# Fourth layer's stack put in order by ScalarE in 16 pieces instead of by two GpSimd copies

## The reference

```
q, k, v = (qkv[:, :, 0], qkv[:, :, 1], qkv[:, :, 2])          # (n, t, h, d)
attn = jnp.einsum('nthd,ntkd->nthk', q * scale, k)            # 16 x 16 for each token
attn = jax.nn.softmax(attn, axis=-1)
out = jnp.einsum('nthk,ntkd->nthd', attn, v)
out = out.transpose(0, 2, 1, 3).reshape(n, t, d)
```

## Time and profile before

| | |
|---|---|
| median of 3 runs | 1935.79 us (1934.92 to 1936.99) |
| the profiled execution | 1931.41 us, span 1929.6 us |
| PE busy | 1609.7 us (83%) |
| DVE busy | 1265.1 us (66%) |
| ACT busy | 934.0 us (48%) |
| POOL busy | 382.1 us (20%), of it 112.4 us in 16 copies of line 571 |
| mean granted clock of TensorE | 0.875 of full speed |

### The profile page before, as it was taken

One profiled execution on the slowest core, in us unless ns is written; L12 is line 12 of the kernel. 1 busy time (PEld: TensorE's weight loads), 2 busy tenths in 40 slices (PEclk: granted clock), 3 DMA queues, 4 the chain that ended last, 5 costly groups with the idle time before them and its releaser, 6 DMA issues. The chain is left out here.

```text
span 1929.6 us, 37580 instructions
## 1 busy us (share of the span) xinstructions
PE 1609.7 (83%) x13794; PEld 1045.1 (54%) x13794; DVE 1265.1 (66%) x3174; ACT 934.0 (48%) x2095; POOL 382.1 (20%) x432
## 2 busy tenths in 40 slices
PE   7357977977888999999898998989878777977888
PEld 4124544554455666666666666656555455555556
DVE  5664666576577767666767767676676677566743
ACT  0124445544555555555555556555444444443544
POOL 1020111011021111111111111111331434143310
PEclk9957777878899999998989989899788789787978
DMA  6150331232144433333333434343675777557530
GB/s 175 49 142 21 95 81 40 69 94 58 38 116 102 100 94 97 95 95 92 97 91 98 97 98 100 92 102 92 52 104 89 80 64 105 89 71 66 109 10 25
DMA packets 198009, 163.22 MB, mean 85 GB/s; under 512 B 80108, under 2 KB 182004, under 8 KB 191684
## 3 DMA queue, kind: packets, MB, share of 16 engines
q1 hardware_dynamic: 189444, 153.14, 40.7%
q10 hardware_dynamic: 8384, 7.69, 1.4%
HBM read 98.05 MB, written 61.95 MB: 83 GB/s over the span
## 5 line engine op out<-in xcount | busy, mean ns | idle before, releaser
L1052 DVE TENSOR_REDUCE maxima<-score_bank 128x4 f32<-128x512 f32 x512 | 339.3, 686 | 141.1 <-PE score_bank L1338 140.4
L777 ACT ACTIVATE p_room<-st_bank 128x512 f32<-128x512 f32 x512 | 299.4, 597 | 231.5 <-PE st_bank L1363 146.4
L1363 PE MATMUL st_bank<-stack_room 64*128 64x128 bf16 x2048 | 243.9, 234 | 43.6 <-DMA stack_room<-max_T 25.6
L1363 PEld LDWEIGHTS st_bank<-stack_room 64*128 64x128 bf16 x2048 | 147.2, 101 | 203.2 <-issue 138.7
L1421 PE MATMUL lin<-h2T,w_h 128*128 128x256 f32 (+1 forms) x640 | 223.3, 444 | 30.6 <-ACT h2T L667 17.6
L835 ACT ACTIVATE gelu<-lin 128x256 f32<-128x256 f32 (+1 forms) x320 | 119.0, 382 | 264.2 <-PE lin L1421 264.2
L1338 PE MATMUL score_bank<-stack_room 62*128 62x128 bf16 x2048 | 201.7, 227 | 8.5 <-DVE maxima L1052 5.8
L563 POOL TENSOR_TENSOR part_low<-qk_rest,part_mid 96x512 bf16<-96x512 f32 x96 | 116.9, 1218 | 437.8 <-DVE part_mid L1038 437.8
L1447 PE MATMUL lin<-w_f,gelu 128*128 128x144 f32 (+1 forms) x1280 | 190.0, 296 | 0.0
L1074 DVE RECIPROCAL o_recip<-o_bank 128x16 f32<-128x16 f32 x128 | 32.8, 256 | 234.6 <-PE o_bank L1391 234.6
L549 POOL TENSOR_TENSOR rstd<-var,neg_half 128x2 f32<-128x2 f32 (+1 forms) x96 | 77.1, 803 | 534.3 <-DVE var L912 299.3
(11 more groups left out here) (194 smaller groups left out, 2719.1 us busy)
## 6 DMA issues: line engine op xcount, KB each, us to landing
stack_room<-stack_dram SPq DMA_DIRECT2D x96, 512.0 KB, 7.6
gates<-gates_dram SPq DMA_DIRECT2D x64, 288.0 KB, 4.3
stack_dram<-part_high SPq DMA_DIRECT2D x64, 288.0 KB, 3.1
norm_room<-stack_dram SPq DMA_DIRECT2D x32, 512.0 KB, 8.1
stack_dram<-part_mid SPq DMA_DIRECT2D x64, 192.0 KB, 2.6
stack_dram<-part_high SPq DMA_DIRECT2D x64, 144.0 KB, 3.2
stack_dram<-part_mid SPq DMA_DIRECT2D x64, 96.0 KB, 2.8
stack_dram<-part_low SPq DMA_DIRECT2D x64, 96.0 KB, 2.1
```

Of the source, the lines that this page charges most:

```text
L777: eng.activation(probs[:, i % PBUFS, :], st_bank[i % 2][:, :], ACT.Exp, scale=float(HD) ** -0.5)\
L1052: eng.tensor_reduce(maxima[:, b, CH * c:CH * c + CH], score_bank[i % 2][:, :].rearrange("p (h k) -> p h k", h=CH), AX_X, ALU.max)\
L1363: ins = eng.matmul(o, score_columns(1, g, b, c, j, HALF), score_columns(0, g, b, c, j, HALF), start=True, stop=flow_of(g) == "a")
```

## The change

GpSimd's `reorder` is deleted. ScalarE gets one that does the same permutation in 16 pieces, 8 for each of the two tiles: a piece takes 16 of the 128 values of m with all 32 of c, that is one run of 512 elements of stage, and writes them to the stack 256 bytes apart (the next m goes 2 bytes further). Pieces 0 to 7 of group L run in body(g): one after each of the five GELUs of half h = 1, and three at the end of the body behind the two `copy_max`. Pieces 8 to 15 run in the next body, one in each of the attention steps 0, 1, 5, 7, 10, 11, 13 and 15. Each piece first waits that the stage of its group is loaded. The stack that they write was last read by group g = L - 2, whose shifted scores are all done before its GELUs. The counts of `reordered` and the waits on it go from 2 to 16.

```diff
+PIECES = 8
-    "v_mixed": 2, "reordered": 2,
+    "v_mixed": 2, "reordered": 2 * PIECES,
@@ SP, load_stack
-                need(eng, "reordered", L - 1, 1)
+                need(eng, "reordered", L - 1, 2 * PIECES - 1)
@@ GpSimd
-            def reorder(J):
-
-                need(eng, "stack_loaded", J, STACK_LOADS - 1)
-                need(eng, "st_done", J - 2, STEPS - 1)
-                for s in range(2):
-                    eng.tensor_copy(stack[J % 2][s].rearrange("p (c m) -> p c m", m=TOK),
-                                    stage[s].rearrange("p (m c) -> p c m", m=TOK)).then_inc(S["reordered"], 1)
-                if J < NG and flow_of(J) == "t":
-                    reorder(J)
@@ ScalarE
+            def reorder(g, pieces):
+
+                need(eng, "stack_loaded", g, STACK_LOADS - 1)
+                n = TOK // PIECES
+                for i in pieces:
+                    k, s = divmod(i, 2)
+                    eng.activation(stack[g % 2][s].rearrange("p (c m) -> p m c", m=TOK)[:, k * n:(k + 1) * n, :],
+                                   stage[s].rearrange("p (m c) -> p m c", m=TOK)[:, k * n:(k + 1) * n, :], ACT.Copy)\
+                       .then_inc(S["reordered"], 1)
@@ ScalarE, attention(g)
+                rest = iter(range(PIECES, 2 * PIECES) if g + 1 < NG and flow_of(g + 1) == "t" else ())
+                    if i in (0, 1, 5, 7, 10, 11, 13, 15):
+                        for piece in rest:
+                            reorder(g + 1, [piece])
+                            break
@@ ScalarE, body(g): behind each GELU, and at the end
+                        if h == 1 and L < NG and flow_of(L) == "t":
+                            reorder(L, [T])
+                if L < NG and flow_of(L) == "t":
+                    reorder(L, range(FCT, PIECES))
@@ PE, scores
-                    need(eng, "reordered", g, 1)
+                    need(eng, "reordered", g, 2 * PIECES - 1)
```

## The result

The changed kernel takes 2051.6 us in the median (2046.7 to 2060.6), the kernel before 1936.4: a ratio of 1.059 (95% interval 1.054 to 1.064), slower by 115 us. Forecast were 1870 us, with a range of 1840 to 1912. The profiled execution took 2060.6 us, span 2058.9.

What follows compares the result with a forecast made beforehand. Layer 3's bodies (65.0 us, no engine full) were taken as bound by a VectorE cast held by GpSimd's copies. Savings of 48, 4 and 14 us less 0.5 gave 1865.9, plus 4.4 for the median: 1870 us, range 1840 to 1912.

Steps and rivals of the forecast that it cites:

- The hold: In layer 3's bodies with copies, GpSimd's two copies hold a VectorE cast 9.6 to 12.5 us; the change removes this.
- The body without additions: A layer 3 body without the copies, before ScalarE's added work: 22 us to exponential 15 plus 28.4, 50.4 us.
- The price of a piece: Each of 128 ScalarE copies of 512 elements: 0.62 us alone, 0.5 in a row, at most 1.04.
- The third rival: Pieces dearer still, kernel slower than before from about 1.1 us a piece; 1978 us at 1.46; chance 0.06.
- The rule of the 16-byte line: Skill text cited against the 0.62 us: writes going to a new SBUF line with each element should be slower.
- the doubled price: Second rival: ScalarE's pieces cost 1.04 us, 0.95 in a row, giving 1912 us; chance 0.25.
- The chain and the wait: SP's values, parts and stage loads end 47.2 us into a body; ScalarE waits 3.4 us; bodies 57 us.
- The clock: PE's granted clock in layer 3's bodies was to rise above 0.83.

Runs made afterwards that it cites:

- e5: The kernel before with GpSimd's two copies cut down to 8 elements each, nothing added on ScalarE (stack not put in order): 1817.7 us, ratio 0.940.
- e2: The changed kernel with each of the 16 pieces writing its 512 elements in a row (stack not put in order): 1880.0 us, ratio 0.972 to the kernel before.
- e8: The changed kernel with each piece writing its 512 elements in a row, run once more for its profile: 1863.6 us.
- e9: The changed kernel with two neighbours of the stack written one after the other within each piece: 1874.0 us, ratio 0.967 to the kernel before.

## Why the prediction was wrong

**The hold: right.** In the kernel after, the casts take 174 ns and PE doesn't wait at the flip, and in e5 exponential 0 to 15 takes 22.6 us (1519.72 to 1542.35) where I took 22. The body without additions was to be 50.4 us, and 51.0 were measured.

**The price of a piece: the step that failed.** The sum took 0.62 us for a piece and bounded it by 1.04 "from above"; it is 2.51. The upper end was built as twice ACT's time for an element, and that is what a jump costs in a read or in float32 (1.06 to 1.13). For single bf16 writes it isn't an upper end at all, and no row of the trace bore on them: GpSimd's 1.72 ns an element, which I set beside it, came from reads 64 bytes apart with writes in a row, and line 667's runs of 16 are the case that is free. I read both as evidence on a write that neither makes. The third rival, slower from about 1.1 us a piece and 1978 us at 1.46, was the right mechanism with a chance of 0.06. By its own sum with the measured price, 128 x (2.51 - 0.62) = 242 us on 1870, nothing hidden, it would have given 2112; 2052 were measured, so a part was hidden. With the same pieces at 0.62 to 0.68 us (e2, e8, e9) the kernel takes 1864 to 1880: the price alone turned the sign.

**The rule of the 16-byte line: right in direction, in part wrong in detail.** The Trainium skill, "Advanced Engine Details and Errata", section "SBUF Cachelines", says that going to another 16-byte line with each access costs a penalty, and that two hits on a line absorb the access time. It names no price; the doubling was mine. The traces agree for reads and float32 writes (0.69 us at 8 bytes apart, 1.13 at 16) and for pairs (0.63 to 0.67). They differ for single bf16 writes: at 8 bytes apart two of them hit each line, and they cost 1.38 us against 0.66 in a row. That the page speaks against this change deserved more than 0.25, and that the range ended at the doubled price was the error that no row excused.

**The chain and the wait: right in sum by luck.** At the price taken, bodies took 57.3 us (57 forecast), but not as forecast. ACT waited 1.1 to 1.7 us for the stage in four of those six bodies of e8 and not at all in the other two, where I had 3.4 in each. Its attention part took 27.8 us in body(27) (1600.12 to 1627.93), and 26.5 to 28.1 in the others, instead of my 24.2. The two errors cancel. Against e5's 22.6 us the added work cost some 5 us there and not the 2.2 that I gave it, and so the work came almost as late as the DMA. In body(23) ACT waited 6.4 us. In the kernel after, the wait came once, 2.2 us: pieces four times as long leave nobody early.

**The clock: wrong in direction.** I had counted on a clock above 0.83, and it fell to 0.67. One body of the kernel after in four stretches (columns as in rows 1): the end of the MLP, the last products and first scores, PE's wait, and what follows.

```profile
1683.00:1695.00 12.00, 8.98 (x45) 5.58 (x45) 5.32 (x12) 11.21 (x10) 0.79 (x1) 0.75 0.01 1
1695.00:1702.90 7.90, 7.90 (x55) 6.15 (x54) 3.92 (x8) 6.33 (x7) 1.31 (x5) 0.50 0.00 0
1702.90:1710.90 8.00, 0.06 (x2) 0.05 (x1) 0.00 (x0) 7.95 (x7) 0.00 (x0) 0.50 0.36 111
1710.90:1723.00 12.10, 11.58 (x91) 7.79 (x91) 5.47 (x13) 8.71 (x12) 0.00 (x0) 0.50 0.55 14
```

PE is at the lower of its two levels already ahead of the wait of 7.9 us, behind the GELUs where pieces leave it idle for a quarter of the time, and stays there through the wait and the 12 us behind it. PE's busy time for six bodies is 378.5 us against 276.1 in e5, for the same products. How much of that 102 us lies on the path no run separates.

## What to carry to other kernels

Price an access pattern by both of its sides and by its type: on this chip a bf16 write of single elements, 16 bytes or more apart, cost about four times a write in a row on ScalarE, GpSimd and VectorE (2.5 us for 0.66, 2.54 for 0.68, 1.34 for 0.33), while on ScalarE pairs in an aligned 4-byte word cost nothing extra (0.63 to 0.67); an order of loops that keeps two neighbours together saved 178 us here. Where no row shows a pattern, its price has no upper end, and a sum in which it occurs 128 times mustn't be given a narrow range. And a long GpSimd copy that stands in VectorE's way need not move: cut into 16 pieces with a wait ahead of each, which leaves 0.06 us between them, it gave back 5.5% of the time, and without the waits 0.6%.

## What the runs showed of the hardware

- Single bf16 writes of 512 elements on ScalarE: 0.66, 0.81, 1.38, 2.55 us at 2, 4, 8, 16 bytes apart, no dearer up to 512. By the last three, about 4.5 ns for each stretch of 16 bytes visited (an estimate). GpSimd takes 2.54 us at 16 bytes and more, VectorE 1.34 against 0.33 in a row.
- Reads and float32 writes on ScalarE: 0.69 us at 8 bytes apart, 1.06 to 1.13 from 16 on.
- Bf16 runs of 2, 256 bytes apart: 0.65 us from an even element, 1.66 from an odd one.
- Reads that alternate between two places 64 bytes apart, moving on by one element each: 0.69 us, where a read that moves on by 64 bytes with each element costs 1.09.
- A cast on VectorE is held through 16 separate GpSimd copies that follow each other without a gap (12.7 us), and for at most 1.03 us if each copy waits for the one before (gaps of 0.06 us).
